# Gated attention: VectorE's normalisation and ScalarE's square at other places of a chunk

## The reference, cut to what matters

```
S = S * exp(g_t) + k_t v_t^T          o_t = q_t S
layer 0:  o = o * sigmoid(gate);  o = o * rsqrt(mean(o*o per head) + eps)
layer 1:  o = o * rsqrt(mean(o*o per head) + eps) * silu(gate)
x = x + ga * (o @ Wo)
```

## Time and profile before

| | us |
|---|---|
| median of three executions (lowest, highest) | 3150.76 (3150.07, 3151.40) |
| the profiled execution's own time | 3150.11 |
| span of its profile | 3148.3 |
| busy in the span: PE | 2853.6 |
| busy in the span: DVE | 2314.3 |
| busy in the span: ACT | 1970.9 |
| busy in the span: POOL | 1226.9 |

### The profile page before, as it was taken

The page is one execution under the profiler, slowest core; times in us unless marked ns, Lnnn a source line. Parts: engine busy times, 40 slices in busy tenths (PEclk is TensorE's granted clock), DMA queues, the critical chain, the costliest instruction groups (busy, mean ns, idle before and its releaser), DMA issues.

```text
span 3148.3 us, 88094 instructions
## 1 busy us (share of the span) xinstructions
PE 2853.6 (91%) x36283; PEld 1716.4 (55%) x36340; DVE 2314.3 (74%) x4012; ACT 1970.9 (63%) x5637; POOL 1226.9 (39%) x911
## 2 busy tenths in 40 slices
PE   5689888778898899999599999999999999999997
PEld 4444577523345233333366666666666666666664
DVE  5740487289703777776688888888888888888885
ACT  4532464174222466666388888877888878888785
POOL 0110012000000111110377766776766676676662
PEclk7589955889899799999799999999999999999999
DMA  2000000000000200000322323233222332322222
GB/s 108 3 1 1 38 4 3 1 0 0 1 0 19 59 24 23 23 22 10 123 69 67 81 69 90 67 81 102 67 70 69 102 81 61 97 69 67 65 60 51
DMA packets 48239, 153.40 MB, mean 49 GB/s; under 512 B 11552, under 2 KB 13856, under 8 KB 45952
## 3 DMA queue, kind: packets, MB, share of 16 engines
q1 hardware_dynamic: 47872, 148.17, 17.9%
HBM read 43.60 MB, written 5.44 MB: 16 GB/s over the span
## 4 chain that ended last, share of the span: by engine, by line
PE 70%; DVE 16%; ACT 8%; issue 3%; DVEq 2%; DMA 1%; ACTq 0%; POOLq 0%; POOL 0%; SPq 0%
PE ps L1627 14%; PE ps L756 7%; PE ps L1645 5%; PE ps L1680 5%; DVE arena L1127 4%; PE ps L1222 4%; PE ps L1250 4%; PE ps L1689 4%; PE ps L1702 4%; PE ps L1237 3%; PE ps L1662 3%; PE ps L1671 3%; PE ps L1708 2%; DVE arena L2095 1%; PE ps L1654 1%
## 5 line engine op out<-in xcount | busy, mean ns | idle before, releaser
L1627 PE MATMUL ps<-arena 128*128 128x512 f32 x1152 | 563.3, 611 | 16.8 <-ACTq L1914 16.4
L1979 ACT ACTIVATE arena<-ps,arena 128x64 f32<-128x64 f32 x1536 | 458.8, 318 | 86.1 <-DVE arena L2175 82.5
L2252 POOL TENSOR_TENSOR arena<-arena 128x1024 f32<-128x1024 f32 x190 | 447.4, 2360 | 97.8 <-DVE arena L2064 97.8
L2258 POOL TENSOR_TENSOR arena<-arena 128x2048 f32<-128x2048 f32 x95 | 344.3, 3624 | 225.1 <-ACT arena L1921 220.2
L1387 DVE TENSOR_REDUCE arena<-ps 128x1 f32<-128x512 f32 x512 | 329.5, 686 | 76.8 <-PE ps L1222 71.7
L1349 ACT ACTIVATE arena<-ps 128x1024 f32<-128x1024 f32 x256 | 262.2, 1024 | 178.3 <-PE ps L1237 169.6
L1979 ACT ACTIVATION_READ_ACCUMULATOR arena<-ps,arena 128x1 f32 x1536 | 323.3, 211 | 0.0
L1627 PEld LDWEIGHTS ps<-arena 128*128 128x128 f32 x1152 | 197.5, 191 | 182.4 <-issue 157.7
L191 POOL TENSOR_SCALAR rstd<-mv 128x4 f32<-128x4 f32 x32 | 8.1, 252 | 681.6 <-DVE mv L178 681.6
L2059 DVE TENSOR_TENSOR arena<-ps,arena 128x1024 f32<-128x1024 f32 x192 | 234.2, 1220 | 47.0 <-PE ps L1627 32.7
L2064 DVE TENSOR_TENSOR arena<-ps,arena 128x512 f32<-128x512 f32 x384 | 245.6, 682 | 0.0
(11 more groups left out here) (286 smaller groups left out, 5532.4 us busy)
## 6 DMA issues: line engine op xcount, KB each, us to landing
arena<-pack_l SPq DMA_DIRECT2D x144, 256.0 KB
arena<-grow SPq DMA_DIRECT2D x144, 256.0 KB
arena<-in_deep SPq DMA_DIRECT2D x6, 2649.5 KB, 11.0
arena<-pack_l SPq DMA_DIRECT2D x96, 128.0 KB
arena<-grow SPq DMA_DIRECT2D x84, 128.0 KB
arena<-in_rotary SPq DMA_DIRECT2D x6, 1024.0 KB, 7.4
pack_tern<-in_tern SPq DMA_DIRECT2D x2, 2888.0 KB, 10.2
arena<-scr_q SPq DMA_DIRECT2D x96, 48.0 KB
```

Of the source, the lines that this page charges most:

```text
L1627: last = T.matmul(m.ps[0:rows.stop - rows.start, at + half, :], f.xs[t % 2][:, rows], w.wqkv[:, j * INNER + half * BLK:j * INNER + (half + ...
L1979: last = A(f.prob[:, p, :], m.ps[:, 4 + j % 2, i * SPAN:(i + 1) * SPAN], ACT.Exp, bias=f.nmax[t % 2][:, p:p + 1], accum_out=f.rsum[t % 2][ ...
L2252: G.tensor_tensor(f.rot[t % 2][:, here], f.rot[t % 2][:, here], f.sin[:, here], ALU.add)
L2258: G.tensor_tensor(r, r, spread(f.ss[t % 2], DH), ALU.mult).then_inc(s["rotated"], 1)
```

## The change

On VectorE, in both layers, `summed(n-1)` and `normed(n-2)` stand behind the filler of the chunk and no longer ahead of it. On ScalarE, in layer 0 alone, the square of chunk n-1 stands ahead of the second exponentials and no longer behind them. No instruction is added or taken away, and no semaphore count changes.

```diff
@@ gla_scalar, loop over chunks @@
         for pair in range(pairs):
             picks(n, pair)
+        if g.layer == 0 and n:
+            squares(n - 1)
         if quarter >= 1:
             decays(quarter + 1, ahead[2:])
         if g.layer == 1:
             squares(n)
-        elif n:
-            squares(n - 1)
         if quarter == 0:
             decays(quarter + 1, ahead)
@@ gla_vector, loop over chunks @@
             done.then_inc(s["state"], 1)
             dve.drain()
 
-        if n:
-            summed(n - 1)
-        if n >= 2:
-            normed(n - 2)
         if quarter + 1 < TILES // CHUNKS:
             if c4 == 0:
                 differences(quarter + 1, [*(LEVEL_OPS if quarter == 0 else LEVEL_OPS[4:]), 1])
@@
         if quarter + 2 < TILES // CHUNKS and c4 == CHUNKS - 1:
             differences(quarter + 2, LEVEL_OPS[:4])
+        if n:
+            summed(n - 1)
+        if n >= 2:
+            normed(n - 2)
     gated(TILES - 1)
```

## The result

The changed kernel takes 3133.85 us (median of five, 3131.76 to 3137.47), the kernel before in the same five rounds 3150.76 us (3148.96 to 3152.71). The ratio is 0.9948, with a 95% interval of 0.9936 to 0.9959. The profiled execution took 3133.27 us with a span of 3131.5.

A forecast was written before the change was run, and what follows sets the result against it. Layer 0 was taken as held up by VectorE's waits for ScalarE's square. 12.5 less 0.6 gives 11.9 us; 3150.11 less 11.9 is 3138.2, with 0.65 for the median 3138.9; range 3136.5 to 3142.8.

The forecast's parts named there:

- The waits (part 1): VectorE, layer 0, chunks 1 to 10: filler ahead of the sum removes 12.5 of 13.5 us of waits for ScalarE's square.
- What is late next (part 2): Layer 0's state update against TensorE's update matmul: 0.12 us slack; new waits in chunks 2 and 8 return 0.6 us.
- The first rival: TensorE takes part back: layer 0's picks-to-update chain 0.5 us longer, six chunks lose 2.6 us, 3141.5 us; chance 0.12.
- ScalarE's part (3): Layer 0, chunks 4, 5, 8, 9: square ahead of second exponentials is worth nothing on top of VectorE's filler.
- Layer 1 (5): Layer 1's loop: new order worth zero, as VectorE doesn't wait for a square; bounds 0.4 us less to 1.0 more.
- After the loop (6): Stages behind layer 0 start when it ends, nothing in them overlaps it; the gain is passed on in full.
- the prediction's own sign of being wrong: Wrong if state-update waits reach several us, layer 1 changes over 1 us, or a stage behind layer 0 changes length.
- The third rival: Higher clock level comes later in the feed-forward stage behind layer 0; at 36 us of delay 3157 us; chance 0.02.
- The second rival: Layer 0's filler, moved away, escapes GpSimd's collisions of 0.69 us a chunk: 6.9 us more gain, 3132 us; chance 0.02.
- The fourth rival: Layer 0's VectorE wait only moves, to filler whose products need exponentials; time stays at 3150 us; chance 0.03.

The follow-up runs named there:

- the kernel before with two products: The kernel before plus two drained, otherwise useless VectorE products (1.5 us of delay) behind layer 0: 3149.72 us, ratio 0.9996.
- GpSimd's version: The changed kernel with the multiplication by 1/rms on GpSimd, behind its power, in both layers: 3139.20 us, ratio 0.9963.

## Why the prediction was wrong

**The waits (part 1) were right.** The ten waits are gone, and so are 12.07 us from mask product 1 to 11; the sum had 11.9.

**What is late next (part 2) was right**, down to the slack of a chunk (0.12 us forecast, 0.09 measured) and the new waits in chunk 8 (0.47 and 0.60) and chunk 2 (0.1 and 0.12). The first rival, TensorE taking part of it back, falls.

**ScalarE's part (3) was right:** nothing beside VectorE's, and 5.2 us alone, shown by two kernels with each half of the change. **Layer 1 (5) was right:** zero, shown from both sides. Its reading of the waits left one out: in 411 to 495.3 us of the kernel before VectorE waits twice for the update matmul, 1.2 us and

```profile
DVE arena L630 <- PE ps L332: 0.8, 1, 0.8
```

Neither is for a square, so nothing hangs on it. One line in layer 1's waits of the changed kernel could mislead there; it is shown with the two instructions behind its longest wait:

```profile
ACT arena L464 <- DVE arena L589: 4.1, 2, 3.1
```

```profile
419.39 0.41 DVE L589 TENSOR_REDUCE arena<-arena 128x4 f32<-128x256 f32 x1
```

```profile
419.88 0.38 ACT L464 ACTIVATE arena<-ps 128x256 f32<-128x256 f32 x1 [3.14 <-DVE arena L589]
```

The square of chunk 3 seems to wait for the moved sum. By the code it needs the sum that VectorE made one chunk earlier; this one only ended (419.80) at about the time when TensorE's output did. The square stands 419.88 - 412.41 = 7.47 us behind its chunk's mask product, and so it did before (435.11 - 427.64). A releaser is inferred from times; the distance to something that can't have moved tells whether it is one.

**After the loop (6): this step failed.** It said that the stages behind layer 0 start sooner and nothing else, and passed the gain on in full; a change of their length stood in the sum at nothing. In the runs the time of the kernel does not follow the start of the later stages one to one: within one group, 12.3 us of delay cost 16.8 us, and 6.9 us of delay made the kernel 2.7 us faster than 5.4. In the changed kernel 4.8 us came on top of the loop's 12.1, and the prediction's own sign of being wrong, that a stage behind layer 0 changes its length, was there: 41.59 instead of 43.59 us at the front of layer 1. That the granted clock carries it is shown where equal work was compared: at the front of layer 1 (41.6 to 45.3 us, at 0.91 down to 0.80), behind layer 1's feed-forward matmuls (4.1 us, TensorE's busy time 4.8 us less), and in the last stretch of the kernel (95.3 to 99.9 us, TensorE's busy time 76.40 to 80.98).

**The third rival named this mechanism and had it one-sided**: only as a loss, only in the feed-forward stage behind layer 0, and to be decided by a single delay of 24 us or more. What the runs show in its place is many small ones, of either sign, at the fronts and ends of the stages, one of the largest (4.6 us) in the last 100 us of the kernel. I took the 1.3 us by which three executions differed as a sign that the clock did not matter. Five executions of the kernel before already lie 3.8 us apart, and a range for the scatter of a median and for the stages behind should have had some 5 us on both sides.

**The second rival**, 6.9 us more for collisions with GpSimd that go away, gave a time (3132) near the measured one for a reason that isn't there: in the loop, where these collisions would be, the forecast without them holds to 0.2 us.

**The fourth rival**, that the wait is only moved, falls with the first.

**Open.** ScalarE's part gave 4.9 and 10.4 us with the same code, layer 0's first mask product starts anywhere from 73.7 to 76.4 us in the profiled executions though no edit lies ahead of it, and the kernel before with two products gained 2.8 us though the front of layer 1 was slower in its profiled execution (45.22 us) than in that of the kernel before (43.59), so the shift does not decide alone. How much of the 4.8 us would come back if the changed kernel were measured again is therefore not known; VectorE's part alone and in layer 0 alone, with the same loop, gave 3.5 and 4.8. Why the instants at which the level changes should keep step with the kernel's stages from one execution to the next, so that medians of several executions differ at all, no run shows. Nor was it tried to hold the clock at one level.

## What to carry to other kernels

Cost a change in an early stage by its own stage, and give the sum a margin for the stages behind, in both directions: here some 5 us on either side of 3150. Look at the single executions before the median, since it can sit at the edge of one of two clusters. Before a gain or a loss beyond the working is put down to the edit, compare the same stretch in untouched stages, with its granted clock, and run a variant that does the same edit and shifts the rest by a few us of idle work. When an engine waits for another engine's late result, put work that doesn't need the result ahead of the wait; here this move of the reader made the move of the producer worthless.

## What the runs showed of the hardware that was not expected

More idle work in an early stage can leave the kernel faster. Nine VectorE products of 0.766 us each behind layer 0 took 3140.26 us and seven took 3142.96, side by side; behind it is TensorE's clock in later stages, at the front of layer 1 0.86 and 0.80 on average over the same 250 matmuls. GpSimd's version with and without two products (3135.22 and 3139.20 us) points the same way, measured in different groups. The Trainium skill, TensorE: Matmul & The Clock Gate, "Part 1: The HAM clock gate (the "warmup" mystery)", says that the point at which the clock rises varies from run to run, at a cost under 1% of a kernel. The page means the rise at a kernel's start; here the trace of the changed kernel has over twenty stretches at 0.50 in one execution. The size agrees: 5 us are 0.16% of this kernel. That executions of one and the same code fall into clusters (3132 to 3134 and 3140 us in VectorE's part alone, 3139 to 3142 and 3145 to 3148 in ScalarE's), and that repeated medians can land on different ones, is what these runs add.

Once at 0.50 in layer 1's loop, TensorE did not rise from it until the loop's last mask product in any of the kernels, busy for 94% of the stretch of chunks 1 to 10, 79.3 of 84.3 us, with mostly small matmuls.
